# The sort of the edges is finished ahead of the first normalisation, and the paced edge writes of GpSimd may run twelve columns further ahead

## The chip, the cores and the metric

The kernel runs on one NeuronCore of a Trainium2 chip. The metric is the device time of one execution in microseconds (us). The engines are named as in the profile: PE is TensorE, DVE is VectorE, ACT is ScalarE, POOL is GpSimd and SP is SyncE. DVEq, ACTq, SPq and POOLq are their queues, in which waits, semaphore and DMA-issuing instructions stand.

## What is computed

The reference is a stack of four blocks over 1250 nodes of width 1024, each added to its input. Each block normalises its rows first. The first block is an edge-weighted graph convolution, the second a mixture of four experts of which two are used, the third a relational graph convolution with gating over eight relations, the fourth a mixture of eight experts. Only the first block and the edge list matter here:

```python
src, dst = edges sorted by dst          # 21250 edges, a type and a weight for each
h    = sigmoid(layernorm(x) @ wenc.T + benc)          # 1250 x 500
h2   = h @ conv_weight
agg  = segment_sum(h2[src] * edge_weight[:, None], dst)
x    = x + (agg + h @ lin_weight.T) @ wdec.T + bdec
```

## The kernel before

Rows are held in ten tiles of 128 nodes (`NT`). The 21250 edges lie in SBUF as 128 partitions by 167 columns (`ET`). They are sorted into 184 slots of 128 edges (`SLOTS`); a pair of slots belongs to one node tile, so that a slot can be summed with one matrix product. Every later gather uses the sorted list.

**The sort.** `sort` on DVE (lines 2081 to 2120) makes a one-hot of the tile of each edge, scans it and hands the counts to PE (`counts_ready`). PE answers with two small products of ten columns (lines 1043 and 1044). In between DVE runs what is given as `between`: here `first_ln`, the statistics (line 2055) and the scale factors of the first normalisation for all ten tiles. Only then does DVE wait for PE's answer (`dve.wait_ge(v_full, full + 1)`), and computes from it the place of every edge, lines 2099 to 2120, then `slot_groups` and lines 2158 to 2169. At `v.sem_inc(scatter_ready, 1)` each edge has a lane and a slot.

**Two ways into the list.** The sorted list is built in two halves. The first 67 columns (`PERMUTED`) go through PE: for each, DVE makes three one-hot products (`permute`, lines 2178 to 2180, written to tiles that the trace calls room) and counts up `perm_ready`; PE multiplies them into a PSUM bank (line 1057, two matmul records for each column) and counts up `perm_done`. DVE may be four columns ahead of PE. The other 100 columns (`SCATTERED`) are written by POOL into a list in DRAM, one indirect DMA for each column (line 905). POOL starts when the list has been cleared (`list_zero`, a DMA that SP issues at line 634 behind the loads of inputs and weights) and `scatter_ready` is up. It is paced by `perm_ready`: before every fourth write from the ninth on it waits until DVE has made `written // 2 - 3` columns. So two writes go with each column that DVE makes.

**The encoder.** ACT turns the statistics of DVE into a square root (line 1558), normalises each tile (line 1562), and copies what PE has transposed (line 1034) out of PSUM (line 1554). Once four tiles are transposed, PE starts the encoder product (line 1079): twelve groups (three groups of nodes by four blocks of the embedding), each of eight steps, each group followed by a sigmoid of ACT (line 1599). Behind the first two groups PE puts one column of the list (line 1057) between the steps. Some groups are followed by the transposes of further tiles (`LN1_AFTER`), and a transpose may only run when ACT has copied the one before it. The encoder is followed on PE by the product with the convolution weights (line 1098, 80 matmuls), whose rows ACT stores to DRAM (line 1612). POOL waits for all of these stores and then gathers rows by the list, one indirect DMA for each slot (line 914). That DVE has the list ready before then (line 2188 on) is needed too.

The order of the work on each engine is the order in which it is written out.

Of the kernel before, what the change touches and what calls it, by code (L numbers as in the profile page):

```python
# [30 lines left out]
P = 128  # L31
N_NODES = 1250
D = 1024
NT = -(-N_NODES // P)
# [9 lines left out]
ET = -(-N_EDGES // P)  # L44
# [81 lines left out]
V_PRE = 0  # L126
# [48 lines left out]
def build(nc, a, out):  # L175
    ctx = ExitStack()
    with ctx:
# [3 lines left out]
        def sem(name):  # L181
            return ctx.enter_context(nc.semaphore(name))
# [111 lines left out]
        def scratch(n):  # L294
            used[0] += n
            assert used[0] <= KE * NPAD
            return lane[:, used[0] - n:used[0]]
# [7 lines left out]
        e_key = scratch(ET)  # L305
        e_hot = scratch(NT * ET)
        e_cum = scratch(NT * ET)
        e_pos = scratch(ET)
        e_lane = scratch(ET)
        e_slot = scratch(ET)  # L310
# [118 lines left out]
        a_bank, v_bank, t_bank = banks[0:2], banks[2:4], banks[4:6]  # L429
# [44 lines left out]
        perm_ready, perm_done = sem("perm_ready"), sem("perm_done")  # L474
# [36 lines left out]
        def rows_of(m):  # L511
            return P if m < NT - 1 else LAST
# [367 lines left out]
        def _(pool):  # L880
# [19 lines left out]
            pool.wait_ge(scatter_ready, 1)  # L900
            for t in range(ET - SCATTERED, ET):
                written = t - (ET - SCATTERED)
                if written >= 8 and written % 4 == 0:
                    pool.wait_ge(perm_ready, written // 2 - 3)
                pool.indirect_dma_start(list_dram, bass.IndirectOffsetOnAxis(ap=e_at[:, t:t + 1], axis=0),  # L905
                                        e_rec[:, t, :], None).then_inc(scattered, 16)

# [1134 lines left out]
        def _(dve):  # L2042
# [4 lines left out]
            def link(ins):  # L2047

                steps[0] += 1
                ins.then_inc(dve_step, 1)  # L2050
                dve.wait_ge(dve_step, steps[0])

            def ln_stats(m):
                for h in range(2):
                    last = v.bn_stats(stats[:, m % 2, h, :], X[:, m, h * HALF:(h + 1) * HALF])
                link(last)
                return v.bn_aggr(mv[:, m, :], stats[:, m % 2, :, :].rearrange("p a b -> p (a b)"))
# [13 lines left out]
            def tile_scale(m, base):  # L2071

                dve.wait_ge(std_tile_ready, base + m + 1)
                link(v.reciprocal(rstd[:, m:m + 1], std[:, m:m + 1]))
                v.scalar_tensor_tensor(nmr[:, m:m + 1], mv[:, m, 0:1], -1.0, rstd[:, m:m + 1], ALU.mult, ALU.mult).then_inc(rstd_tile_ready, 1)

            def sort(key, groups, cols, onehot, cum, pos, bank, full, tmp, far, between=lambda: None, rows=P, least=0):


                gs = slice(0, groups)  # L2080
                shape = [P, groups, cols]
                by_group = lambda ap: ap.rearrange("p (g t) -> p g t", t=cols)
                wide = cols < P
                if wide:
                    last = v.tensor_tensor(by_group(onehot), key.unsqueeze(1).broadcast_to(shape),
                                           iota_free[:, gs].unsqueeze(2).broadcast_to(shape), ALU.is_equal)
                else:
                    for g in range(groups):
                        last = v.tensor_scalar(onehot[:, g * cols:(g + 1) * cols], key, float(g), None, ALU.is_equal)
                link(last)  # L2090
                link(v.tensor_tensor_scan(cum, onehot, onehot, 0.0, ALU.add, ALU.max))
                ends = cum.rearrange("p (g t) -> p g t", t=cols)[:, :, cols - 1]
                v.memset(pre[:, 2, 0:1], 0.0)
                v.tensor_copy(pre[:, 2, 1:groups], ends[:, 0:groups - 1])
                link(v.tensor_copy(pre[:, 0, gs], ends))
                v.tensor_tensor(pre[:, 1, gs], pre[:, 0, gs], pre[:, 2, gs], ALU.subtract).then_inc(counts_ready, 1)
                between()
                dve.wait_ge(v_full, full + 1)
                link(v.tensor_scalar(prei[:, 0, gs], bank[:, 16:16 + groups], float(rows - 1), None, ALU.add))
                link(v.tensor_scalar(prei[:, 1, gs], prei[:, 0, gs], rows.bit_length() - 1, None, ALU.arith_shift_right))  # L2100
                link(v.tensor_scalar(pre[:, 4, gs], prei[:, 1, gs], float(rows // P), None, ALU.mult))
                if least:
                    link(v.tensor_scalar(pre[:, 4, 0:least], pre[:, 4, 0:least], 1.0, None, ALU.max))
                link(v.tensor_tensor_scan(pre[:, 5, gs], pre[:, 4, gs], pre[:, 4, gs], 0.0, ALU.add, ALU.max))
                link(v.tensor_tensor(pre[:, 6, gs], pre[:, 5, gs], pre[:, 4, gs], ALU.subtract))
                link(v.scalar_tensor_tensor(pre[:, 7, gs], pre[:, 6, gs], float(P), bank[:, 0:groups], ALU.mult, ALU.add))
                v.sem_inc(v_read, 1)
                link(v.scalar_tensor_tensor(pre[:, 3, gs], pre[:, 7, gs], 1.0, pre[:, 2, gs], ALU.subtract, ALU.subtract))
                if wide:
                    v.scalar_tensor_tensor(tmp, key, float(groups), far, ALU.is_ge, ALU.mult)  # L2110
                    link(v.tensor_tensor(by_group(cum), by_group(cum), pre[:, 3, gs].unsqueeze(2).broadcast_to(shape), ALU.add))
                    link(v.tensor_tensor(onehot, cum, onehot, ALU.mult))
                else:
                    for g in range(groups):
                        part = slice(g * cols, (g + 1) * cols)
                        last = v.scalar_tensor_tensor(onehot[:, part], cum[:, part], pre[:, 3, g:g + 1], onehot[:, part], ALU.add, ALU.mult)
                    v.scalar_tensor_tensor(tmp, key, float(groups), far, ALU.is_ge, ALU.mult)
                    link(last)
                link(v.tensor_reduce(pos, onehot.rearrange("p (g t) -> p t g", t=cols), AX.X, ALU.add))
                link(v.tensor_tensor(pos, pos, tmp, ALU.add))  # L2120

            def slot_groups(out_i, tmp, n, groups):

                link(v.tensor_scalar(tmp, iota_free[:, 0:n], pre[:, 5, 0:1], None, ALU.is_ge))
                for g in range(1, groups):
                    link(v.scalar_tensor_tensor(tmp, iota_free[:, 0:n], pre[:, 5, g:g + 1], tmp, ALU.is_ge, ALU.add))
                link(v.tensor_scalar(out_i, tmp, float(groups - 1), None, ALU.min))
# [18 lines left out]
            def first_ln():  # L2146
                for m in range(NT):
                    if m in (0, 4, NT - 1):
                        dve.wait_ge(x_in[(0, 4, NT - 1).index(m)], 16)
                    ln_stats(m).then_inc(x_tile_ready, 1)  # L2150
                    if m >= 1:
                        tile_scale(m - 1, 0)
                tile_scale(NT - 1, 0)

            sort(e_key, NT, ET, e_hot, e_cum, e_pos, v_bank[0], V_PRE, e_lane, e_slot, first_ln, 2 * P)
            slot_groups(l_tile[:], l_tmp[:], SLOTS, NT)

            link(v.tensor_copy(e_t0, e_pos))
# [9 lines left out]
            v.tensor_copy(e_rec[:, :, 1], e_w)  # L2168
            link(v.scalar_tensor_tensor(e_at, e_lane, float(SLOTS), e_slot, ALU.mult, ALU.add))
            v.sem_inc(scatter_ready, 1)  # L2170
            dve.wait_ge(list_zero, 16)


# [317 lines left out]
            for m in range(NT):  # L2491
                rows = slice(0, rows_of(m))
# [418 lines left out]
```

## Time and profile before

| | |
|---|---|
| median of 3 runs | 2619.59 us (2610.77 to 2620.92) |
| the profiled execution | 2613.38 us, of which the span of the profile is 2611.6 us |
| busy PE / DVE / ACT / POOL over the span | 2363.0 / 1623.0 / 993.7 / 885.2 us |
| first edge write of POOL, end of the last | 47.4 us, 189.0 us |
| first column of the list on PE, last encoder matmul ends | 47.8 us, 213.4 us |

The page counts from the start of the span. An idle time stands in front of an instruction and is put down to the semaphore event that came last before it; "remote" is an event for which the profile has no instruction at that time, and "issue" is a wait for nothing that the profile shows. A granted clock (PEclk) of 1.0 is 2.4 GHz and 0.5 is 1.2 GHz.

### The profile page before, as it was taken

The numbers are of one execution on the slowest core, as the hardware profiler recorded it, in microseconds if no ns is written. First come the engines' busy times: TensorE is split into PE (matmuls) and PEld (weight loads), VectorE is DVE, ScalarE is ACT, GpSimd is POOL, SyncE is SP. The second block draws the span as 40 slices with busy tenths as digits, with TensorE's granted clock in tenths as the row PEclk, the third lists the DMA queues.
The fourth block names the chain that finished last, engine by engine and source line by source line (L and its number), as shares of the span: only waits on it lengthen the run. The fifth ranks groups of instructions, "written<-read, shape, count | busy, mean of one in ns | idle before, by whom it ended". The sixth has DMA issues, their size and how long they took to land.

```text
span 2611.6 us, 30845 instructions
## 1 busy us (share of the span) xinstructions
PE 2363.0 (90%) x10104; PEld 1779.6 (68%) x10104; DVE 1623.0 (62%) x2527; ACT 993.7 (38%) x1763; POOL 885.2 (34%) x843
## 2 busy tenths in 40 slices
PE   6578788897999979999999999999899898995998
PEld 3234233365787758877788888888777676874886
DVE  8243566756546447655455455457888889775665
ACT  4001122334334334312212212216788887544333
POOL 2651666600111215565520000014345563211543
PEclk9789899998999989999999999999999998997999
DMA  4002666623555447543533543537777786438884
GB/s 153 1 4 104 184 177 180 176 74 114 172 149 174 155 176 258 179 168 120 190 140 121 189 145 116 201 136 245 237 254 266 282 307 226 161 119 294 299 313 178
DMA packets 196050, 466.18 MB, mean 179 GB/s; under 512 B 29704, under 2 KB 30472, under 8 KB 195928
## 3 DMA queue, kind: packets, MB, share of 16 engines
q1 hardware_dynamic: 98248, 213.31, 23.5%
q0 software_dynamic: 64272, 190.20, 22.9%
q10 hardware_dynamic: 33408, 61.13, 6.2%
q8 instruction: 65, 1.06, 0.2%
q14 instruction: 57, 0.47, 0.1%
HBM read 364.20 MB, written 105.98 MB: 180 GB/s over the span
## 4 chain that ended last, share of the span: by engine, by line
PE 78%; DVE 9%; DMA 4%; issue 4%; another core or an unknown queue 3%; ACT 2%; DVEq 1%; POOL 0%; ACTq 0%; SPq 0%; POOLq 0%
PE pair L1377 8%; PE pair L1375 8%; PE pair L1376 8%; PE pair L1116 4%; PE pair L1393 3%; PE pair L1396 3%; PE pair L1413 2%; PE pair L1414 2%; PE pair L1415 2%; DVE U L2228 2%; PE pair L1098 2%; PE pair L1079 2%; PE pair L1261 2%; PE pair L1263 2%
## 5 line engine op out<-in xcount | busy, mean ns | idle before, releaser
L1554 ACT ACTIVATE sq_h<-quad 128x512 fp32r<-128x512 f32 x196 | 121.7, 632 | 461.7 <-PE pair L1377 411.3
L972 POOL DMA_INDIRECT rows_y<-y_rows,l_row x184 | 208.8, 1135 | 210.4 <-PE pair L1396 181.4
L1375 PE MATMUL pair<-sq_h,xh 128*128 128x512 f32 x700 | 273.6, 391 | 6.4 <-DVE sq_l L2549 4.6
L1376 PE MATMUL pair<-sq_h,xl 128*128 128x512 f32 x700 | 272.4, 389 | 0.0
L1377 PE MATMUL pair<-sq_l,xh 128*128 128x512 f32 x700 | 272.4, 389 | 0.0
L2637 DVE SCALAR_TENSOR_TENSOR low_y<-rows_y,l_inv,high_y 128x1024 fp32r<-128x1024 f32 x184 | 234.4, 1284 | 47.9 <-ACT high_y L1554 44.0
L914 POOL DMA_INDIRECT XT<-h_rows,l_src x184 | 177.5, 965 | 151.3 <-DMA h_rows<-OS 63.1
L1554 ACT ACTIVATE high_y<-rows_y,l_inv 128x1024 fp32r<-128x1024 f32 x184 | 210.5, 1144 | 41.7 <-PE pair L1396 26.5
L949 POOL DMA_INDIRECT inv_ring<-inv_count,at_ring x184 | 191.2, 1039 | 74.7 <-issue 56.2
L2549 DVE TENSOR_TENSOR sq_l<-quad,sq_h 128x512 fp32r<-128x512 f32 x196 | 131.1, 696 | 105.7 <-ACT sq_h L1554 83.8
L1116 PE MATMUL pair<-XT,XN 128*128 128x504 f32 x368 | 196.5, 669 | 0.0
L2228 DVE TENSOR_TENSOR U<-pair,U 128x512 f32 x184 | 127.0, 690 | 109.6 <-PE pair L1116 62.6
L1375 PEld LDWEIGHTS pair<-sq_h,xh 128*128 128x128 f32 x700 | 131.4, 188 | 38.1 <-DVE sq_l L2549 8.3
L963 POOL COPY X<-bias_u 128x1024 f32<-128x1024 f32 x10 | 10.7, 1123 | 418.9 <-PE pair L1377 418.9
L1377 PEld LDWEIGHTS pair<-sq_l,xh 128*128 128x128 f32 x700 | 131.4, 188 | 27.5
L1376 PEld LDWEIGHTS pair<-sq_h,xl 128*128 128x128 f32 x700 | 131.4, 188 | 26.6
L1393 PE MATMUL pair<-high_y,hot 128*128 128x512 f32 x368 | 117.7, 401 | 27.7 <-DVE low_y L2637 27.5
L1554 ACT ACTIVATE XN<-hot,l_w 128x128 f32<-128x128 bf16 x184 | 59.5, 389 | 214.0 <-DVE hot L2215 109.1
L1413 PE MATMUL pair<-wh,xh 128*128 128x512 f32 x320 | 126.4, 395 | 2.0 <-DVE wl L2692 1.9
L1414 PE MATMUL pair<-wh,xl 128*128 128x512 f32 x320 | 125.9, 393 | 0.0
L1415 PE MATMUL pair<-wl,xh 128*128 128x512 f32 x320 | 125.8, 393 | 0.0
L905 POOL DMA_INDIRECT list_rows<-e_rows x100 | 95.9, 959 | 86.5 <-DVEq L2170 40.8
(391 smaller groups left out, 5595.6 us busy)
## 6 DMA issues: line engine op xcount, KB each, us to landing
quad<-in_L_gnn_weight SPq DMA_DIRECT2D x28, 1024.0 KB
xh<-sum_parts SPq DMA_DIRECT2D x14, 1280.0 KB
xl<-sum_parts SPq DMA_DIRECT2D x14, 1280.0 KB
y_rows<-u ACTq DMA_DIRECT2D x70, 256.0 KB
tok_raw<-in_L_ffn_w SPq DMA_DIRECT2D x8, 2048.0 KB
tok_raw<-in_L_ffn_w SPq DMA_DIRECT2D x16, 1024.0 KB, 13.2
x_rows<-X SPq DMA_DIRECT2D x20, 512.0 KB, 6.4
pair<-pair_rows SPq DMA_DIRECT2D x18, 512.0 KB
```

Source lines behind the costliest of these rows:

```text
L949: pool.indirect_dma_start(inv_ring[:, k:k + 1], None, inv_rows, bass.IndirectOffsetOnAxis(ap=at_ring[:, 0, k:k + 1], axis=0)).then_inc(inv ...
L972: pool.indirect_dma_start(rows_y[s % RING1][:], None, y_rows, bass.IndirectOffsetOnAxis(ap=l_row8[:, s:s + 1], axis=0)).then_inc(y_in[s % ...
L1116: mm(sum_bank[s % 4][:, 0:EMBC], hot[:, s % RING, :], rows_h2[:, s % RING0, 0:EMBC], start=True, stop=True).then_inc(slot_summed, 1)
L1375: mm(o, high[:, k, :], sq_h[:, k, :], start=(k == 0), stop=False)
L1376: mm(o, low[:, k, :], sq_h[:, k, :], start=False, stop=False)
L1377: last = mm(o, high[:, k, :], sq_l[:, k, :], start=False, stop=(k == KE - 1))
L1393: mm(o[:, cols], hot_s, high[:, cols], start=first, stop=False)
L1413: mm(o, xh[:, m, k, :], wh[:, k, :], start=(k == 0), stop=False)
L1414: mm(o, xl[:, m, k, :], wh[:, k, :], start=False, stop=False)
L1554: return nc.scalar.activation(dst, src, func, **kw)
L2228: v.tensor_tensor(agg[:, bass.ds(t, 1), :], sum_bank[s % 4][:].rearrange("p (o n) -> p o n", o=1), agg[:, bass.ds(t, 1), :], ALU.add).then ...
L2637: v.scalar_tensor_tensor(low_y[s % RING1][:], rows_y[s % RING1][:], l_inv[:, s:s + 1], high_y[s % 3][:].bitcast(F32), ALU.mult, ALU.subtra ...
```

## The change

`first_ln` is no longer handed to `sort` to be run between the counts and PE's answer. `sort` runs to its end, `slot_groups`, the lanes and slots and `scatter_ready` follow, and then comes `first_ln`, in front of the wait for the cleared list and of the columns. POOL's waits for `perm_ready` begin at the 21st write instead of the ninth, and each asks for six columns fewer, which is twelve writes. Nothing else differs; the number of instructions of each engine stays, less the three waits of POOL at 8, 12 and 16 writes.

```diff
--- before.py
+++ after.py
@@ -900,8 +900,8 @@
             pool.wait_ge(scatter_ready, 1)
             for t in range(ET - SCATTERED, ET):
                 written = t - (ET - SCATTERED)
-                if written >= 8 and written % 4 == 0:
-                    pool.wait_ge(perm_ready, written // 2 - 3)
+                if written >= 20 and written % 4 == 0:
+                    pool.wait_ge(perm_ready, written // 2 - 9)
                 pool.indirect_dma_start(list_dram, bass.IndirectOffsetOnAxis(ap=e_at[:, t:t + 1], axis=0),
                                         e_rec[:, t, :], None).then_inc(scattered, 16)
 
@@ -2152,7 +2152,7 @@
                         tile_scale(m - 1, 0)
                 tile_scale(NT - 1, 0)
 
-            sort(e_key, NT, ET, e_hot, e_cum, e_pos, v_bank[0], V_PRE, e_lane, e_slot, first_ln, 2 * P)
+            sort(e_key, NT, ET, e_hot, e_cum, e_pos, v_bank[0], V_PRE, e_lane, e_slot, rows=2 * P)
             slot_groups(l_tile[:], l_tmp[:], SLOTS, NT)
 
             link(v.tensor_copy(e_t0, e_pos))
@@ -2168,6 +2168,7 @@
             v.tensor_copy(e_rec[:, :, 1], e_w)
             link(v.scalar_tensor_tensor(e_at, e_lane, float(SLOTS), e_slot, ALU.mult, ALU.add))
             v.sem_inc(scatter_ready, 1)
+            first_ln()
             dve.wait_ge(list_zero, 16)
```

## Rows read from the trace of the kernel before

**Rows 1.** The page, part 4: the chain that ended last, shares by engine.

```profile
PE 78%; DVE 9%; DMA 4%; issue 4%; another core or an unknown queue 3%; ACT 2%; DVEq 1%; POOL 0%; ACTq 0%; SPq 0%; POOLq 0%
```

**Rows 2.** Busy time of each engine in one stretch; columns stand in its first line.

```profile
core 0: us, PE busy (x) PEld busy (x) DVE busy (x) ACT busy (x) POOL busy (x), PEclk, DMA share, GB/s
...
47.78:213.97 166.19, 117.62 (x318) 62.78 (x317) 74.54 (x214) 11.98 (x19) 95.52 (x100) 0.84 0.02 2
```

**Rows 3.** Waits, 28 to 252 us: waiter <- releaser: total us, times, longest.

```profile
ACT U L1599 <- remote: 61.2, 2, 38.4
...
DVE room L2178 <- remote: 52.8, 8, 15.0
PE pair L1057 <- DVE room L2180: 44.8, 9, 11.9
...
POOL list_rows L905 <- DVE room L2180: 16.4, 3, 7.3
```

**Rows 4.** Timeline of DVE: start, duration, instruction, count, [idle before <- releaser].

```profile
13.16 1.28 DVE L2055 BATCH_NORM_STATS2 stats<-X 128x6 f32<-128x512 f32 x2
...
30.01 0.16 DVE L2075 SCALAR_TENSOR_TENSOR nmr<-mv,rstd 128x1 f32<-128x1 f32 x1
30.08 0.16 DVE L2099 TENSOR_SCALAR prei<-pair 128x10 int32<-128x10 f32 x1
...
46.62 0.35 DVE L2178 TENSOR_SCALAR room<-pair,U 128x128 f32<-128x128 f32 x1
```

**Rows 5.** Timeline of PE, 13 to 214 us.

```profile
13.81 0.58 PE L1044 MATMUL pair<-pre,ones 128*128 128x10 f32 x2
...
28.48 7.11 PE L1079 MATMUL pair<-XT,W 128*128 128x512 f32 x16 [0.83 <-ACT XT L1554]
...
47.78 0.88 PE L1057 MATMUL pair<-room 128*128 128x368 f32 x2
...
60.57 0.78 PE L1057 MATMUL pair<-room 128*128 128x368 f32 x2
...
207.58 5.77 PE L1079 MATMUL pair<-XT,W 128*128 128x256 f32 x26
```

**Rows 6.** Timeline of SP: the issues that clear the DRAM list and read it back.

```profile
31.25 0.43 SPq L634 DMA_DIRECT2D list_rows<-room  x1
190.16 0.32 SPq L637 DMA_DIRECT2D XN<-list_rows  x1
```

**Rows 7.** DMA issues, 30 to 47 us: the last number is us to landing.

```profile
list_rows<-room SPq DMA_DIRECT2D x1, 184.0 KB, 3.0
```

**Rows 8.** Timeline of POOL: the first and last write and those after a pause.

```profile
47.41 1.12 POOL L905 DMA_INDIRECT list_rows<-e_rows  x1 [40.77 <-DVEq L2170]
...
105.03 0.96 POOL L905 DMA_INDIRECT list_rows<-e_rows  x1 [7.27 <-DVE room L2180]
...
138.75 0.96 POOL L905 DMA_INDIRECT list_rows<-e_rows  x1 [3.73 <-DVE room L2180]
...
174.16 0.96 POOL L905 DMA_INDIRECT list_rows<-e_rows  x1 [5.42 <-DVE room L2180]
...
188.04 0.95 POOL L905 DMA_INDIRECT list_rows<-e_rows  x1 [0.30 <-issue]
```

**Rows 9.** Timeline of DVE, 59 to 104 us: permutes and the idle time before them.

```profile
59.04 0.35 DVE L2178 TENSOR_SCALAR room<-pair,U 128x128 f32<-128x128 f32 x1 [0.37 <-PE pair L1057]
...
68.66 0.35 DVE L2178 TENSOR_SCALAR room<-pair,U 128x128 f32<-128x128 f32 x1 [8.51 <-remote]
...
97.35 0.35 DVE L2178 TENSOR_SCALAR room<-pair,U 128x128 f32<-128x128 f32 x1 [10.10 <-remote]
...
103.65 0.35 DVE L2178 TENSOR_SCALAR room<-pair,U 128x128 f32<-128x128 f32 x1 [5.20 <-remote]
```

**Rows 10.** Timeline of ACT, 63 to 104 us.

```profile
63.72 0.60 ACT L1554 ACTIVATE XT<-pair 128x512 f32<-128x512 f32 x1 [2.24 <-remote]
...
103.81 0.69 ACT L1599 ACTIVATE U<-pair,b_enc 128x512 f32<-128x512 f32 x1 [38.37 <-remote]
```

## The prediction

> **What bounds the kernel now.** I read the chain that ended last first: 78% of it is PE and nothing of it POOL or a queue of DVE [rows 1]. So the change counts only as far as it moves PE, and it works in the first tenth of the span. The stretch to look at is that from PE's first column of the list (47.78 us) to the end of the encoder (207.58 + 5.77 = 213.35 us) [rows 5]. In it PE is busy for 117.62 of 166.19 us, at a mean granted clock of 0.84 [rows 2]. PE idles 48.6 us there, and of the busy time about 0.16 x 117.6 = 18.8 us are owed to the clock at its lower level; together some 67 us are lost. What follows (the convolution product, the stores, POOL's gathers) starts when the encoder is done and moves with it. The time of the change is therefore the shift of the encoder's end.
>
> Next I read who waits for whom in the stretch. PE waits for DVE's columns (44.8 us in 9 times), DVE for "remote" (52.8 us in 8), ACT for "remote" (61.2 us in 2) [rows 3]. "Remote" is the thing to understand. DVE's column at 68.66 us needs PE's column of 60.57 us, done at 61.35 [rows 5, 9]. DVE was free and the product was done, and still it began 7.3 us later. One such wait before, at 59.04 us, took 0.37 us. ACT's sigmoid at 103.81 us came after 38.37 us of idle, in the same moment as DVE's release at 103.65 [rows 9, 10]. So it is not DVE that is slow: what PE has counted up reaches DVE and ACT late. When? POOL's writes run back to back, 1.26 us each, from 47.41 us; it pauses before the write of 105.03 us (7.27 us idle), of 138.75 (3.73) and of 174.16 (5.42), and ends at 188.99 [rows 8]. The first late release is 13 us into the first burst, the releases get rarer the longer it lasts (the idle times grow from 8.51 to 10.10 us), and the jam clears about 6 us after the burst has stopped at 97.76, at 103.65 [rows 8, 9]. I take this as the law of the stage: some 13 us of a burst of writes are free, then PE's counts come late until a few us after the burst. Why that is so the trace does not show.
>
> **Part 1, the finish of the sort ahead of the statistics.** DVE's statistics run from 13.16 to 30.08 us (16.9 us) and the finish from 30.08 to 46.62 us, where the first column begins (16.5 us) [rows 4]. Swapped, the finish must wait for PE's answer, done at 13.81 + 0.58 = 14.39 us [rows 5]: 1.2 us that the statistics hid before are now open. The finish ends at about 14.4 + 16.5 = 30.9, the statistics at 47.8, and the columns begin 1.2 us later than before. The cost: ACT's square roots, the transposes and the encoder hang on the statistics, so PE's first encoder product moves from 28.48 [rows 5] by 16.5 + 1.2 = 17.7 us to 46.2 us. Nothing hides that, for PE has nothing else to do there. With nothing else changed the first column goes from 47.8 to 65.5 us.
>
> **Part 2, POOL's first write.** The finish would allow it at 30.9 + 0.8 = 31.7 us. (47.41 - 46.62 = 0.8 is taken as the lag.) But POOL waits for the cleared list first, and SP issues that DMA at 31.25 us, with 3.0 us to landing [rows 6, 7]: 34.3 us, taken as 34.5. So the list's clearing is late next, and of 16.5 us only 47.4 - 34.5 = 12.9 us are won for POOL. SP's own queue is not touched: its next wait, for the writes and for the transposes, is over at 190.16 us in before [rows 6] and by the sum at about 195, still in front of the encoder's end. DVE's wait for the cleared list, behind the statistics now, costs nothing, since it is over 13 us earlier.
>
> **Part 3, the waits.** Before, two writes go with one column, and POOL is held three times, 16.4 us [rows 3]. A cycle from one pause's end to the next is 138.75 - 105.03 = 33.7 and 174.16 - 138.75 = 35.4 us, mean 34.6, for 24 writes (POOL stood at 40, 64 and 88) and 12 columns [rows 8]. The new bound is written = 2 x (columns + 9), with the same slope, so a cycle that has begun keeps its length. What changes is where the first hold falls. Up to the 28th write four columns are enough, which DVE makes without PE, from 47.8 us on. The 28th write comes at 34.5 + 28 x 1.262 = 69.8 us and wants five. The fifth needs PE's first column, 65.5 us at the earliest.
>
> **Part 4, what the first burst does to the encoder's opening.** This cost the trace of before does not show, since no write was under way then. The burst now runs from 34.5 to 69.8 us. Thirteen free us end at 47.5, and until the columns PE needs ACT three times: the copies of tile 4's transposes, those of tile 5, those of tile 6. PE's counts for tile 4 fall at 53 to 54 us, in the jam. From below: if they come as before, nothing is lost here, but POOL still stops at 69.8 us and DVE's fifth column waits until the jam clears, up to 75.7 us (5.9 us as after 97.76 [rows 8, 9]). From above: two counts in turn must wait, the second until the jam has cleared, 10 + 10 us by the longest idle time of 10.10 us [rows 9]. I take 12 us, near one wait for a release (8.51) and half of another, as the jam is young at 54 us. So PE's first column is at 65.5 + 12 = 77.5 us, and POOL goes on 2 us later, when PE has done it and DVE has made the fifth: 79.5 us.
>
> **The sum.** From there three cycles of 24 writes take POOL to 100: 79.5 + 3 x 34.6 = 183.3 us, with 41 columns made. Before, that point is at 174.16 us, and the encoder ends 213.35 - 174.16 = 39.2 us later [rows 5, 8]; now there are no writes beside it, but that rest held hardly a loss before (its burst is 14.8 us long, of which 13 are free). 183.3 + 39.2 = 222.5 us against 213.35: 9.1 us later. With the bounds of part 4: 75.7 + 103.8 + 39.2 = 218.7 (5.3 us later) and 85.5 + 2 + 103.8 + 39.2 = 230.5 (17 us later). The profiled execution is 2613.4 us, so it would be 2622.5; it lies 6.2 us below the median of the runs, 2619.6, and on that median I expect 2628.7 us. From DVE, POOL and ACT nothing else is added: no instruction is new.
>
> **Rival 1: the loss follows the overlap (a gain).** POOL finishes earlier, so the columns have more time alone. Before, writes and columns overlap from 47.8 to 189.0, 141 us, and 67 us are lost, 0.48 for each us. If POOL is never held, the writes end at 34.5 + 126.2 = 160.7 us, and the overlap is 160.7 - 65.5 = 95 us, which loses 45. Then 22 us are saved against 17.7 us of later start: 4 us faster, 2615. Should the looser waits also do away with the 16.4 us of holding on top, 21 us faster, 2599. For it: POOL's end is not bound by PE then. Against it: the pauses are what clears the jam [rows 8, 9], so fewer of them should cost.
>
> **Rival 2: the loss stays with the columns (slower).** PE loses 67 us in a stretch of 166 us whatever POOL does. Then all 17.7 us of the later start remain: 2637 us. The place is PE's first encoder product, the price the shift of DVE's statistics, and it decides when writes under way before the first column spare the columns nothing. The upper bound of part 4 ends in the same place. The page SBUF — State Buffer of the Trainium skill, section Who interferes with whom, says that PE and ACT never wait on anyone for SBUF and that DMAs do not contend with compute. By that rule the bursts would not be what delays PE, and this rival would hold. The trace speaks against the conclusion: the long idle times begin and end with the bursts [rows 8, 9], though by another way than a port perhaps.
>
> **Rival 3: the change does nothing.** The encoder's later start is just what the jam of the first burst (40 writes, 57.6 us, before) cost, and both cancel: 2619.6.
>
> **How the numbers follow.** Forecast (5 to 12 us slower) 0.45; rival 1 0.27, of which its far part 0.14; rival 2 and the upper bound 0.22; rival 3 0.06. About 0.5%, 13 us, is what a measurement of this kernel can tell from no change. The forecast and rival 3 are within it (0.51), of rival 1 the near part (0.13); rival 2 with the upper bound, at 17 to 18 us, is beyond (0.22). That gives faster 0.14, same 0.64, slower 0.22. The range takes in most of rival 1 and rival 2 with the spread of the runs: 2602 to 2643 us.
>
> **What would show it.** Part 1: DVE's statistics from 30.9 to 47.8 us, the first encoder product at 46.2. Part 2: POOL's first write at 34.5, not at 31.7. Part 3: a first hold of POOL before its 29th write (69.8 us) and three or fewer cycles of some 34 us after. Part 4: ACT's copies of tiles 4 and 5 with idle times put down to "remote" of 5 us and more. The sum: POOL's last write near 179 and the encoder's end near 222 us. Wrong it would be if DVE's columns are released within 0.4 us while a burst is older than 13 us, if POOL is not held at its 29th write, or if the first column stands at 65.5 us and the encoder ends before 213.

## The result

| | before | changed |
|---|---|---|
| median of 9 runs (lowest to highest) | 2619.59 us (2610.77 to 2625.54) | 2625.95 us (2622.85 to 2632.21) |
| ratio to before, 95% interval | | 1.0039 (1.0023 to 1.0056) |
| span of the profiled execution | 2611.6 us | 2626.4 us |
| first edge write of POOL / first column on PE / encoder's end | 47.4 / 47.8 / 213.4 us | 33.8 / 86.9 / 228.2 us |

The change makes the kernel slower by 0.39%, some 10 us by the ratio and 6.4 us by the medians. The two traces differ by 14.8 us, and all of it stands at the encoder's end: 228.20 against 213.35 us. POOL's first gather comes 14.8 us later as well (266.91 against 252.07), and its last output write too. What lies behind the encoder is only shifted. Each trace is of one execution: that of before ran 6.2 us below its median, that of the changed kernel (2628.17 us) 2.2 us above, which is why the traces lie further apart than the runs.

The chain that ended last, in the page of the changed kernel, has PE with 81% where before it was 78% [rows 1]:

```profile
PE 81%; DVE 7%; DMA 4%; another core or an unknown queue 3%; issue 3%; ACT 1%; DVEq 0%; POOL 0%; ACTq 0%; SPq 0%; POOLq 0%
```

Busy time of each engine from the old place of the first column to the new one, and from there to the encoder's end (columns in the first line):

```profile
core 0: us, PE busy (x) PEld busy (x) DVE busy (x) ACT busy (x) POOL busy (x), PEclk, DMA share, GB/s
47.78:86.86 39.08, 21.39 (x61) 11.10 (x60) 5.92 (x19) 11.65 (x17) 16.32 (x17) 0.87 0.01 1
86.86:228.20 141.34, 111.33 (x317) 61.18 (x315) 72.56 (x205) 11.31 (x18) 69.15 (x72) 0.87 0.02 2
```

Before, there was one stretch of 166.19 us in which PE was busy for 117.62 [rows 2], of which 165.6 us lie ahead of the encoder's end. The stretch with the columns is now 141.3 us long with 111.3 us of PE work, so it has become shorter by 24.2 us, and 39.1 us in front of it have been added.

The timeline of PE in the changed kernel, the lines that answer to [rows 5]:

```profile
54.35 9.09 PE L1079 MATMUL pair<-XT,W 128*128 128x512 f32 x16 [6.07 <-issue]
...
75.94 1.94 PE L1034 MATMUL pair<-ident,XN 128*128 128x128 f32 x8 [11.62 <-ACT XT L1554]
...
86.86 0.78 PE L1057 MATMUL pair<-room 128*128 128x368 f32 x2
...
222.42 5.78 PE L1079 MATMUL pair<-XT,W 128*128 128x256 f32 x26
```

The timeline of DVE, which answers to [rows 4] and [rows 9]:

```profile
14.44 0.17 DVE L2099 TENSOR_SCALAR prei<-pair 128x10 int32<-128x10 f32 x1 [1.18 <-PE pair L1044]
...
30.94 1.29 DVE L2055 BATCH_NORM_STATS2 stats<-X 128x6 f32<-128x512 f32 x2
...
54.42 0.16 DVE L2074 RECIPROCAL rstd<-std 128x1 f32<-128x1 f32 x1 [5.30 <-issue]
...
87.68 0.35 DVE L2179 TENSOR_SCALAR room<-pair,U 128x128 f32<-128x128 f32 x1 [28.58 <-PE pair L1057]
```

The timeline of ACT, which answers to [rows 10]:

```profile
46.52 0.60 ACT L1554 ACTIVATE XT<-pair 128x512 f32<-128x512 f32 x1 [2.29 <-PE pair L1034]
...
50.76 0.60 ACT L1554 ACTIVATE XT<-pair 128x512 f32<-128x512 f32 x1 [3.46 <-remote]
53.61 0.60 ACT L1554 ACTIVATE XT<-pair 128x512 f32<-128x512 f32 x1 [2.25 <-remote]
...
73.33 1.28 ACT L1599 ACT_TABLE_LOAD   x1 [16.49 <-remote]
```

The timeline of POOL, which answers to [rows 8]: the first and last write and those behind a pause:

```profile
33.84 1.12 POOL L905 DMA_INDIRECT list_rows<-e_rows  x1 [27.19 <-DMA list_rows<-room]
...
68.15 0.96 POOL L905 DMA_INDIRECT list_rows<-e_rows  x1 [0.30 <-issue]
89.06 0.96 POOL L905 DMA_INDIRECT list_rows<-e_rows  x1 [19.95 <-DVE room L2181]
...
123.44 0.96 POOL L905 DMA_INDIRECT list_rows<-e_rows  x1 [4.33 <-DVE room L2181]
...
164.12 0.96 POOL L905 DMA_INDIRECT list_rows<-e_rows  x1 [5.56 <-DVE room L2181]
...
188.16 0.96 POOL L905 DMA_INDIRECT list_rows<-e_rows  x1 [0.30 <-issue]
```

The reader is to see this. POOL writes without a pause from 33.84 to 69.11 us, 28 writes. From 44.0 us on, when that burst is 10.2 us old, ACT gets what PE has done late (2.29, then 3.46, 2.25 and 16.49 us of idle). The second half of tile 2's transposes was done at 44.0 us and is copied at 46.52, 2.5 us later; the two halves of tile 3's were done at 45.46 and 48.29 us and are copied 5.3 us later each. The fourth wait is that of the first sigmoid. It ends at 73.33 us, 4.2 us after the burst has. DVE's statistics wait for ACT's square roots behind those copies (5.30 us of idle at 54.42). PE starts the encoder at 54.35 and not at 46.2 us, idles 11.62 us before the transposes of tile 5, the second of two tiles behind the first group, and reaches its first column at 86.86 us. POOL stands still for 19.95 us meanwhile, because its 29th write wants DVE's fifth column.

### The profile page after: what moved, and what is told of

Read it like the earlier page. It is cut to its first block, busy times and chain, and to the rows that moved or that the text cites. A ratio compares the mean times of both kernels' runs of the same rounds, so it can differ in the third digit from the quotient of the medians.

```text
span 2626.4 us, 30845 instructions
## 1 busy us (share of the span) xinstructions
PE 2358.9 (90%) x10104; PEld 1779.7 (68%) x10104; DVE 1626.0 (62%) x2527; ACT 995.8 (38%) x1763; POOL 889.9 (34%) x843
## 4 chain that ended last, share of the span: by engine, by line
PE 81%; DVE 7%; DMA 4%; another core or an unknown queue 3%; issue 3%; ACT 1%; DVEq 0%; POOL 0%; ACTq 0%; SPq 0%; POOLq 0%
PE pair L1377 8%; PE pair L1375 8%; PE pair L1376 8%; PE pair L1116 5%; PE pair L1393 3%; PE pair L1396 3%; PE pair L1413 3%; PE pair L1415 2%; PE pair L1414 2%; PE pair L1098 2%; PE pair L1079 2%; DVE U L2229 2%; PE pair L1261 2%; PE pair L1263 2%
## 5 line engine op out<-in xcount | busy, mean ns | idle before, releaser
L963 POOL COPY X<-bias_u 128x1024 f32<-128x1024 f32 x10 | 10.7, 1122 | 406.4 <-PE pair L1377 406.4
```

## Experiments

Theory A is that of the prediction: in a burst of POOL's indirect DMAs some 13 us are free, and from then on what PE counts up reaches DVE and ACT late, until a few us after the burst. Each kernel has one trace. The code cuts show only the lines on which a run rests. The rivals are that the loss belongs to PE's columns whatever POOL does (B), that looser waits are a gain (C), and those named with each run.

**The two halves of the change apart.** First the new order with the old waits:

```diff
-                if written >= 20 and written % 4 == 0:
-                    pool.wait_ge(perm_ready, written // 2 - 9)
+                if written >= 8 and written % 4 == 0:
+                    pool.wait_ge(perm_ready, written // 2 - 3)
```

> The new order on VectorE with the old waits of GpSimd. Theory A (long bursts of GpSimd's writes hold back what TensorE counts up): the first burst now stops at its 16th write, about 54 us, instead of the 28th at 69 us, so the jam clears before the encoder's opening is through. First column on TensorE near 71 us instead of 86.9, three cycles of 34.6 us from 73 us, encoder's end near 216 us: 3 us above the kernel before, some 12 us below the changed kernel in the trace. Rival B (the loss belongs to TensorE's columns, whatever GpSimd does): encoder's end 17.7 us later than before, as in any kernel with the new order. Rival C (looser waits are a gain): slower than the changed kernel by up to 16 us, the time for which GpSimd is held.

Measured: 2621.6 us against 2616.97, ratio 1.0013 (0.9994 to 1.0032); encoder's end 215.40 + 5.78 = 221.18 us, 7.8 us later than before. POOL's and PE's timelines:

```profile
49.24 0.96 POOL L905 DMA_INDIRECT list_rows<-e_rows  x1 [4.02 <-DVE room L2181]
...
70.64 0.96 POOL L905 DMA_INDIRECT list_rows<-e_rows  x1 [11.59 <-DVE room L2181]
...
105.07 0.95 POOL L905 DMA_INDIRECT list_rows<-e_rows  x1 [4.39 <-DVE room L2181]
...
145.83 0.95 POOL L905 DMA_INDIRECT list_rows<-e_rows  x1 [5.68 <-DVE room L2181]
```

```profile
47.14 9.09 PE L1079 MATMUL pair<-XT,W 128*128 128x512 f32 x16 [0.83 <-ACT XT L1554]
...
68.44 0.78 PE L1057 MATMUL pair<-room 128*128 128x368 f32 x2
...
215.40 5.78 PE L1079 MATMUL pair<-XT,W 128*128 128x256 f32 x26
```

The old waits hold POOL for 4.02 us before its ninth write and for 11.59 us before its seventeenth. The first column stands at 68.44 us, 3 us behind its undisturbed place of 65.5, instead of 21 us behind it. So the jam of the opening comes from the longer first burst, as A has it; B, which gave 17.7 us, falls. The reading rests on the trace: the time by itself can't be told from that of the kernel before. My figure of 3 us was 5 us too small, since one of the cycles took 28 writes and 40.8 us instead of 24 and 34.6.

Then the old order with the new waits, the same edit made the other way round:

```diff
-                if written >= 8 and written % 4 == 0:
-                    pool.wait_ge(perm_ready, written // 2 - 3)
+                if written >= 20 and written % 4 == 0:
+                    pool.wait_ge(perm_ready, written // 2 - 9)
```

> The old order with waits twelve writes later. Theory A: the first burst, from 47.4 us, is not stopped at its 40th write (97.8 us) but some 16 writes later, about 118 us; the jam lasts as much longer, and the encoder ends about 10 to 15 us later than in the kernel before: 2630 to 2635 us. Rival B: nothing moves, 2620 us. Rival C: up to 16 us faster, 2604 us.

Measured: 2621.17 us against 2616.97, ratio 1.0027 (1.0014 to 1.0041). The encoder ends at 221.34 + 5.78 = 227.12 us, 13.8 us later. DVE and POOL:

```profile
112.72 0.35 DVE L2178 TENSOR_SCALAR room<-pair,U 128x128 f32<-128x128 f32 x1 [10.10 <-issue]
...
119.02 0.35 DVE L2178 TENSOR_SCALAR room<-pair,U 128x128 f32<-128x128 f32 x1 [5.20 <-remote]
```

```profile
47.40 1.12 POOL L905 DMA_INDIRECT list_rows<-e_rows  x1 [40.76 <-DVEq L2170]
...
120.40 0.96 POOL L905 DMA_INDIRECT list_rows<-e_rows  x1 [7.52 <-DVE room L2180]
```

The first burst runs to its 52nd write at 112.9 us instead of the 40th at 97.8, DVE gets one count in 11.2 us for so long, and the jam clears at 119.02 us, 6.1 us after the burst, where before it cleared at 103.65 [rows 9]. The 15 us longer burst is the loss. In time it is 7 us by the ratio (3.7 to 10.7) where the trace has 13.8, less than I had expected; the execution traced, 2634.25 us, was the longest of the ten. Rival C falls: looser waits are a loss by themselves. 1.0013 and 1.0027 together give 1.0040, and the whole change measured 1.0039; with intervals of 0.0013 to 0.0019 to either side that the sum fits so closely is luck.

**The writes left out.** In both orders the 100 writes were taken out, so that 100 of the 167 columns of edges are missing from the list. SP's wait for the writes was replaced by one for the cleared list. The cut is from the new order:

```diff
             for t in range(ET - SCATTERED, ET):
                 written = t - (ET - SCATTERED)
-                if written >= 20 and written % 4 == 0:
-                    pool.wait_ge(perm_ready, written // 2 - 9)
-                pool.indirect_dma_start(list_dram, ...)
```

> The changed kernel with its 100 edge writes left out: the 100 columns of edges that go through DRAM are missing from the list, their places stay zero. All other work is the same. Theory A: no late counts, no idle time of VectorE or ScalarE put down to a remote event between 47 and 200 us; encoder's end near 46.2 + 119 = 165 us, so 63 us less than with the writes, a time near 2563 us. Rival B: TensorE still loses some 67 us beside the columns, encoder's end near 228 us, 2626 us.

> The kernel before with its 100 edge writes left out in the same way. Theory A: encoder's end near 28.5 + 119 = 148 us, 66 us earlier than in the kernel before, and 17.7 us earlier than the same with the new order: this is the price of the new order by itself. Time near 2554 us. Rival B: 213 us and 2620 us as before.

Measured, in one run each: 2576.26 us in the new order and 2545.36 us in the old one (2563 and 2554 expected). PE's last encoder matmuls, first in the new order, then in the old:

```profile
46.26 7.10 PE L1076 MATMUL pair<-XT,W 128*128 128x512 f32 x16 [0.83 <-ACT XT L1551]
...
158.16 5.78 PE L1076 MATMUL pair<-XT,W 128*128 128x256 f32 x26
```

```profile
29.32 7.10 PE L1076 MATMUL pair<-XT,W 128*128 128x512 f32 x16 [0.78 <-ACT XT L1551]
...
141.22 5.78 PE L1076 MATMUL pair<-XT,W 128*128 128x256 f32 x26
```

The encoder ends at 163.94 and at 147.00 us, 64.3 and 66.4 us earlier than with the writes. That is the 67 us which the prediction had read off PE's idle time and clock. Between the orders lie 16.9 us, the bare price of the statistics coming later. That the times differ by 30.9 us and not 16.9 stems from later stages: at POOL's first gather the two are 16.9 us apart, at its last output write 30.9. From the one to the other it takes 2364.4 us in the new order and 2350.4 in the old one, and in the traces of the kernels before and changed 2352.3 and 2352.2 us. The cause of the 14 us stays open, and so the two times are not used here, only the encoder's ends.

**Is GpSimd's work the cause, or its indirect DMAs?** A memset took the place of each write, and SP waited for the memsets instead of the writes:

```diff
-                pool.indirect_dma_start(list_dram, ...).then_inc(scattered, 16)
+                pool.memset(idle_tile[:], 0.0).then_inc(idled, 1)
+                pool.wait_ge(idled, written + 1)
```

> The changed kernel with a memset of 128x1024 on GpSimd in the place of each edge write, at the same pace of 1.27 us and with the same waits for columns; the 100 columns of edges are missing from the list. Theory A in the form that indirect DMAs cause the jam: no late releases, encoder's end near 164 us, 2574 us as without any work on GpSimd. Rival G (that GpSimd is busy without a pause is enough): encoder's end near 228 us as in the changed kernel, 2626 us.

Measured: 2574.92 us in one run. POOL, one of DVE's columns, and PE's end:

```profile
34.71 28.19 POOL L908 MEMSET idle_tile<- 128x1024 f32 x28 [28.07 <-DMA list_rows<-room]
70.53 72.57 POOL L908 MEMSET idle_tile<- 128x1024 f32 x72 [7.63 <-DVE room L2184]
```

```profile
110.93 0.35 DVE L2182 TENSOR_SCALAR room<-pair,U 128x128 f32<-128x128 f32 x1 [0.37 <-PE pair L1060]
```

```profile
161.09 5.78 PE L1082 MATMUL pair<-XT,W 128*128 128x256 f32 x26
```

The encoder ends at 166.87 us, though POOL is busy without a gap for 72.6 us in the second run of memsets. Their pace is 1.01 us each, not the 1.27 that I had expected, so this is no exact copy of the writes in time, but denser. Beside the memsets DVE idles 0.37 us before a column, or 1.25 us where transposes stand in between, and nothing is put down to "remote". It takes the indirect DMAs to hold PE's counts back. Whether it is POOL's making of them or what they set going (their transfers, their own counts) was not tested; the DMA engines are busy for 2% of the stretch with the columns in the kernel before [rows 2] and in the changed one.

**The first write held.** Does it help to keep the burst out of the opening?

```diff
             pool.wait_ge(scatter_ready, 1)
+            pool.wait_ge(perm_ready, 1)
```

> The changed kernel with GpSimd's first write held until VectorE has made its first column (about 49 us). Theory A: the burst is 4 us old when TensorE's counts for tile 4 fall, so the encoder's opening runs undisturbed and the first column stands at 65.5 to 68 us instead of 86.9. But the jam then falls on the columns: the burst isn't held at the 28th write any more, the late releases of VectorE begin at about 62 us and last until a hold near 95 us, and the encoder ends between 220 and 232 us, no earlier than in the changed kernel by more than 8 us. Rival D (the 20 us that the opening lost are gone for good once they are not lost there): encoder's end near 228 - 20 = 208 us, 5 us earlier than in the kernel before.

Measured: 2643.22 us in one run. PE, then POOL:

```profile
46.73 7.11 PE L1080 MATMUL pair<-XT,W 128*128 128x512 f32 x16 [0.78 <-ACT XT L1555]
...
66.03 0.78 PE L1058 MATMUL pair<-room 128*128 128x368 f32 x2
...
228.49 5.78 PE L1080 MATMUL pair<-XT,W 128*128 128x256 f32 x26
```

```profile
49.87 1.12 POOL L906 DMA_INDIRECT list_rows<-e_rows  x1 [43.22 <-DVE room L2182]
...
101.90 0.96 POOL L906 DMA_INDIRECT list_rows<-e_rows  x1 [5.79 <-DVE room L2182]
```

The opening runs undisturbed: first encoder product at 46.73, first column at 66.03 us. The encoder ends at 234.27 us all the same, 6 us later than in the changed kernel and a little above my range, because the jam of 36 writes and more now lies over the columns. Rival D falls. The 21 us of the opening were not an extra: in this one trace the jam costs PE as much beside the columns.

**Pauses by time.** If the length of a burst is what counts, it can be cut without asking for columns. Behind every tenth write come five memsets instead of any wait for columns:

```diff
-                if written >= 20 and written % 4 == 0:
-                    pool.wait_ge(perm_ready, written // 2 - 9)
+                if written and written % 10 == 0:
+                    for k in range(5):
+                        pool.memset(idle_tile[:], 0.0).then_inc(idled, 1)
+                        pool.wait_ge(idled, 5 * (written // 10 - 1) + k + 1)
```

> The changed kernel with GpSimd's waits for the columns taken out and, behind every tenth write, five memsets of 128x1024 on GpSimd in their place: nine pauses of 5 to 6 us, set by time and not by the columns. A burst is then 12.6 us. Theory A: no burst gets old enough for a jam, so TensorE works as without the writes: first column near 65.5 us, encoder's end 165 to 175 us. The writes end at 34 + 126 + 50 = 210 us, later than before, and the list is then what the gather waits for: first gather near 220 us instead of 252, a time some 30 us below the kernel before, 2589 us. Rival E (what counts is how many writes run beside TensorE's work, not how long they run without a pause): the loss stays about 60 us, encoder's end above 215 us, and the time is 2620 us or more.

> As the kernel with pauses, but a pause of two memsets, 2 to 2.5 us, behind every eighth write: bursts of 10.1 us, twelve pauses. Theory A with pauses of this length sufficing to clear what a burst of 10 us has piled up: encoder's end 165 to 175 us, writes end near 190, first gather 203 to 210 us, 42 to 49 us below the kernel before, near 2573 us. If a pause must be 4 us or more to clear it: late releases of 5 us and more return after two or three bursts, the encoder ends above 185 us and the gain is under 25 us. Rival E: 2620 us or more.

> As the kernel with short pauses in the new order, but a pause of four memsets behind every sixteenth write: bursts of 20 us instead of 10, the same sum of pauses. Theory A (what counts is how long a burst lasts, with some 13 us free): late releases come back in the last 7 us of each burst and until the pause has cleared them, the encoder's end moves from 165 us to 185 us or more and the time to 2580 us or more. Rival F (what counts is the mean rate of the writes): encoder's end stays at 165 to 170 us and the time at 2566 us.

Measured: ten writes and five memsets, 2579.72 us, ratio 0.9857 (0.9824 to 0.9889). Eight writes and two memsets, 2565.80 us, ratio **0.9808** (0.9780 to 0.9835). Sixteen writes and four memsets, 2600.91 us in one run. The encoder ends at 170.44, 164.76 and 193.21 us. POOL's pace and PE's end with eight writes and two memsets:

```profile
35.17 1.12 POOL L909 DMA_INDIRECT list_rows<-e_rows  x1 [28.53 <-DMA list_rows<-room]
...
45.12 1.99 POOL L907 MEMSET idle_tile<- 128x1024 f32 x2
47.39 0.96 POOL L909 DMA_INDIRECT list_rows<-e_rows  x1 [0.28 <-POOL idle_tile L907]
...
203.45 0.97 POOL L918 DMA_INDIRECT XT<-h_rows,l_src  x1 [18.74 <-DMA h_rows<-OS]
```

```profile
47.07 7.11 PE L1083 MATMUL pair<-XT,W 128*128 128x512 f32 x16 [0.88 <-ACT XT L1558]
...
66.38 0.78 PE L1061 MATMUL pair<-room 128*128 128x368 f32 x2
...
158.98 5.78 PE L1083 MATMUL pair<-XT,W 128*128 128x256 f32 x26
```

DVE with sixteen writes and four memsets; its burst runs from 59.15 to 79.05 us, the next from 83.32 to 103.22:

```profile
81.83 0.35 DVE L2183 TENSOR_SCALAR room<-pair,U 128x128 f32<-128x128 f32 x1 [21.76 <-PE pair L1061]
...
103.05 0.35 DVE L2183 TENSOR_SCALAR room<-pair,U 128x128 f32<-128x128 f32 x1 [3.09 <-issue]
...
105.87 0.35 DVE L2183 TENSOR_SCALAR room<-pair,U 128x128 f32<-128x128 f32 x1 [1.72 <-PE pair L1061]
```

Pauses of 2.3 us suffice if a burst is 10 us long: the encoder ends 0.8 us after that of the kernel without any writes, and the first gather (203.45 us) waits for the stores of the convolution product, where with the long pauses (216.02 us) it stood behind the writes, which ended at 205.5 us. With bursts of 20 us and nearly the same sum of pauses (6 of 4.3 us instead of 12 of 2.3) DVE's idle times come back in the second half of each burst and PE loses 28 us. Rivals E and F fall: neither the number of the writes nor their mean rate decides, but how long they go on without a break. DVE's idle times beside the columns were of 1 to 3.8 us, as a burst of 20 us is cut before they grow; the opening was hit harder, with PE's first product at 55.32 us behind 8.80 us of idle.

**Which order is better without the jam?** The same pauses in the old order:

> The kernel before with the same pauses of five memsets behind every tenth write, in the old order. Theory A: encoder's end near 148 to 155 us, but the first write is 13 us later than with the new order, the writes end near 225 us and the first gather is near 234 us: 18 us below the kernel before, and 13 us above the new order with these pauses. Here the new order would be the better one, since the writes and not TensorE are late last. Rival E: no gain.

> The kernel before with a pause of two memsets behind every eighth write, in the old order. Theory A: encoder's end near 148 us, the writes end 12 us later than in the new order with the same pauses, near 197 us, and the first gather near 204 us against 203.5: nothing is left of a difference between the orders, 2566 us. Were the new order worth the 13 us by which its writes begin earlier, it would be 2579 us; were it worth less than nothing, as in the first pair, 2550 us.

Measured: 2593.15 us in one run with five memsets behind every tenth write, and 2571.04 us, ratio 0.9816 (0.9794 to 0.9838), with two behind every eighth (2566 expected). The ends of the encoder are 149.19 and 149.33 us. With short pauses POOL's first gather is at 204.41 us and waits for DVE's list, in the new order it is at 203.45 and waits for the stores:

```profile
47.40 1.12 POOL L909 DMA_INDIRECT list_rows<-e_rows  x1 [40.75 <-DVEq L2174]
...
204.41 0.97 POOL L918 DMA_INDIRECT XT<-h_rows,l_src  x1 [7.44 <-DVEq L2203]
```

With long pauses the new order is ahead at the first gather by 225.73 - 216.02 = 9.7 us, as its writes begin earlier. With short ones there is nothing between them, 0.9808 and 0.9816 with intervals that overlap. The old order ends its encoder 15.4 us earlier, but its writes end 12 us later, and DVE's list is what the gather then waits for. They are 1.9% and 1.8% faster than the kernel before.

**The same in the gathers.** Three small memsets behind every tenth of the 184 gathers of rows, on top of the short pauses:

```diff
+                if s and s % 10 == 0:
+                    for k in range(3):
+                        pool.memset(l_inv[:], 0.0).then_inc(idled, 1)
+                        pool.wait_ge(idled, 24 + 3 * (s // 10 - 1) + k + 1)
                 if s >= RING0:
                     pool.wait_ge(slot_summed, s + 1)
```

> The kernel with short pauses in the new order, with the same idea in the stage behind: GpSimd's 184 gathers of rows get three small memsets, some 1.5 us, behind every tenth. Theory A: the late releases of that stage (12.6 us of idle on VectorE once in the kernel before, some of 2 to 3 us) go away, 15 to 20 us, and 18 pauses of 1.5 us cost up to 27 us where the gathers themselves are the bound: the sum lies between 10 us faster and 12 us slower than the kernel with short pauses, so 2556 to 2578 us, 2566 the likeliest. Rival H (the late counts of that stage cost nothing): 25 us slower, 2590 us.

Measured: 2574.83 us, ratio 0.9825 (0.9802 to 0.9849), no better than 0.9808. From the first to the last slot product the stage takes 282 us against 276 without these pauses. The long idle time of DVE in that stage (12.55 us with the short pauses alone) has gone, but others of 2 to 4.3 us remain. A pause is 1.15 us here where 0.30 us would stand between two gathers, some 15 us for 18 of them, and the stage is 6 us longer, so of what they cost part has come back. Rival H's 2590 us did not come, and neither did a gain.

## Why the prediction was right

The change was forecast slower by 9 us, at 2628.7 us; it measured 2625.95 us and 10 us by the ratio.

That 9 and 10 us lie so close is in part luck: in the traces the two are 9.1 and 14.8 us, and two errors of the sum work against each other (part 4).

- **Part 1, right to 0.1 us where nothing disturbs it.** The finish begins at 14.44 us and the statistics at 30.94 (14.4 and 30.9). Their end was not seen right: the last scale factors come at 54.42 and not at 47.8 us, as ACT's square roots stand behind copies that were late. The 17.7 us for the bare shift are 16.9 us between the two kernels without writes.
- **Part 2, right.** The first write is at 33.84 us (34.5) and its idle time is put down to the cleared list, which SP issued 0.7 us earlier than before.
- **Part 3, right on the hold.** The first hold is at the 29th write, at 69.1 us (69.8). Of the three cycles the first took 34.4 us for 24 writes, the second 40.7 for 28, the rest 25.0 for 20; the encoder ends 139.1 us after POOL goes on (143.0). That a cycle keeps its length did not hold for each, only roughly for the three together; POOL's last write ends at 189.1 us and not near 179, as POOL went on 9.6 us late.
- **Part 4 was the mis-sized term.** The 12 us taken for the opening measured 21.4 (86.86 - 65.5), slightly more than the upper bound of 20. It has two parts: PE's first product came 8.1 us late (54.35 for 46.2), as the jam reached the transposes of tiles 2 and 3 already, from 10.2 us into the burst on instead of 13. The prediction had looked for the first loss at tile 4. The way from there to the first column took 32.5 us where before it was 19.3 [rows 5], 13.2 us more. In the trace the sum is therefore 14.8 us instead of 9.1: 9.6 too few in part 4 and 3.9 too many behind it.
- **The signs named.** The copies of tiles 4 and 5 have no wait put down to "remote"; these waits stand before the copies of tile 3 (3.46, 2.25 us) and before the first sigmoid (16.49), and the copies of tile 4 follow it. Of the signs of being wrong none came: no count of a burst older than 13 us released DVE within 0.4 us, POOL was held at its 29th write, and the first column was not at 65.5 us.
- **The law of the stage** was read from the trace of before alone and held in its kind: it takes indirect DMAs, in a row, for more than some 10 us. The 13 us are no fixed number. DVE's column k + 4 needs PE's column k, and paired in this way the first count that comes over 1 us late falls 13.9, 14.0 and 8.9 us into the first three bursts of the kernel before, and 11.3 and 15.0 us into the second and third of the changed one. The third burst of before, begun at 138.75 us, has it in two lines that the prediction did not use: PE's column is done at 147.69 us, DVE takes it up 4.0 us later.

```profile
146.91 0.78 PE L1057 MATMUL pair<-room 128*128 128x368 f32 x2
...
151.67 0.35 DVE L2178 TENSOR_SCALAR room<-pair,U 128x128 f32<-128x128 f32 x1 [5.19 <-PE pair L1057]
```

- **Rival 2** said that PE's loss would not hang on POOL's writes. The two kernels without writes decide against it, 64 and 66 us. The prediction had drawn the same from what the page SBUF — State Buffer of the Trainium skill (section Who interferes with whom) says of PE and ACT never waiting on anyone and of DMAs not contending with compute. The rule itself speaks of the ports of SBUF, and no run here shows that a port is what jams.
- **Rival 1** counted a loss for each us in which writes and columns run together. With short pauses they run together from 66.4 to 184.7 us, 118 us, and the encoder ends 0.8 us later than without writes. Its far part took the waits for a cost. They are the opposite: held POOL is what clears the jam, and setting them later cost 0.27% by itself. **Rival 3** is excluded by the interval.

What stays open is where the counts are held, at PE or on the way. That DVE's and ACT's counts reach others in time in the same microseconds says that it is not every count: in the first burst of the changed kernel ACT's copy is done at 54.21 us and PE starts at 54.35, and ACT's square root, done at 47.30 us, releases DVE at 47.33; in that of the kernel before DVE's column is done at 69.76 us and PE starts on it at 69.81. Whether the smaller differences of the stages behind come from the same jam was not tried apart from the gathers.

## What to carry to other kernels

Where one queue issues indirect DMAs back to back, look at what the others receive from PE in that time, and not only at how long the DMAs take; an idle time put down to nothing in the profile, that grows with the burst and ends with it, is the sign. Cut such a burst by time, into pieces about as long as the shortest time after which a count came late (here 9 us, and pieces of 10 us sufficed), with a pause of 2 us in between, where that queue is ahead of its consumers: here it was worth 50 us, more than any order of the work. A wait that looks like lost time on one engine may be what keeps the others going, so change its place only after leaving out what it paces.

## What was not expected of the hardware

- PE's counts for DVE and ACT come late while POOL issues indirect DMAs in a row at 1.26 us each: on time for the first 9 to 15 us, then one in 3.5, 5, 7, 10.5 and at last 11.2 us, and on time again 3 to 6 us after a burst of 35 us or more. The counts are kept, not lost: that of PE's column done at 65.8 us released DVE at 97.35. 72 memsets in a row, 1.01 us each, did not do this.
- A pause of 2.3 us behind 10 us of writes keeps it away but for a few counts 1 to 2 us late (encoder's end 164.76 against 163.94 us without writes); 4.3 us behind 20 us of writes do not (193.21 us).
- Pauses of 2.3 us twelve times, 27 us of standing still on POOL, made the changed kernel 50 us faster than the one before.
